# Moving one of the five score banks of an attention stage from the maxima tiles to the exponential tiles

## The chip, the cores and the metric

The kernel runs on one core of one Trainium2 chip. The metric is the device time of one execution in microseconds (us), the median of several runs. TensorE (PE; its weight loads, PEld, are listed by themselves), VectorE (DVE), ScalarE (ACT), GpSimd (POOL) and SyncE (SP) each run their own instructions in program order and wait for each other through semaphores. PSUM, into which PE writes its products, is eight banks of 128 partitions x 512 fp32.

## What is computed

Eight sequences of 512 positions with 256 features go through an attention layer and then through a mixture of experts. The part of the reference that matters here is the attention with 16 heads of 16 features:

```python
attn = softmax(einsum('bhid,bhjd->bhij', q, k) / sqrt(16))     # 8 x 16 heads of 512 x 512 scores
mod = attn * coh[..., None]
mod = mod / (mod.sum(-1, keepdims=True) + 1e-08)
mod = (1.0 - fi) * mod + fi * fa[:, None, :, None]
out = einsum('bhij,bhjd->bhid', mod, v)
x = x + out.reshape(...) @ Wout.T + bout
```

After it a gate picks two of eight experts for each row, three layers are computed for the picked ones, and the weighted results are added up.

## The kernel before, in words

`attention` (L180) holds the whole first half, `experts` (L976) the second. The change touches the first alone.

The attention stage is one hand-written sequence of steps s (L621, FIRST to LAST), 16 for each of the eight sequences ("batch" in the code), 128 in all; slot means the step's place within its sixteen (step 54 is slot 6). A step treats four heads of one block of 128 positions. Every head's scores are computed **twice**. An *A tile* (`a_tile`, L426) is a 128 x 512 block of scores with a query position per partition; DVE reduces it to the maximum of each row (`reduce_head`, L746). A *B tile* (`b_tile`, L437) is the transposed block, with the key position per partition, and the maximum already folded into the product; ACT takes its exponential into SBUF (`exps`, L691), and `pv` (L448) multiplies the result with the values. The maxima must be complete before a head's B tiles, so the A tiles run LEAD = 8 steps ahead: in step s PE makes the four B tiles of s and the four A tiles of s + 8. Steps -8 to -1 have A tiles alone (the lead-in, about 52 to 84 us), steps 120 to 127 have B tiles alone (about 629 to 656 us).

The tiles use rings of PSUM banks. A tile number `no` goes to bank `no % RING` of its ring, and PE waits, before it writes, until the tile RING places earlier has been read:

```python
if no >= A_RING:
    pe.wait_ge(a_read, no - A_RING + 1)      # a_tile, L429; the same with b_read and B_RING in b_tile, L440
```

`a_read` is raised by DVE's reduction (L750), `b_read` by ACT's exponential (L697). Before the change the A ring has three banks and the B ring two. Bank 5 gathers the `pv` products, banks 6 and 7 serve all other products of the stage.

PE's order in one step is (L621 to L629):

```python
scores(s, (0, 1))            # B0 A0 B1 A1, called the first pairs below
product(task(s, 0))          # another product of the stage, if PLAN has one here
pv(s - 1)                    # waits until all four exponentials of step s - 1 are done
scores(s, (2, 3))            # B2 A2 B3 A3, the second pairs
product(task(s, 1))
```

A B tile and the A tile that follows it use opposite halves of the array's rows, and start together when neither waits. PLAN (L110) gives the other product of each of the 16 steps, on either side: projections, the coherence layer, transposes, output and gate products. DVE's order (L951 to L969) is two reductions, what it has to take of side 0, two reductions, side 1, and in steps 5, 6, 7, 8, 9 and 11 a piece of the routing of the batch before (`route_batch`, L865), a chain of tiny dependent instructions; the piece of step 9 is the longest (L886 to L891) and ends in `both`, for which the `count` product of step 10 waits. ACT's order (L704 to L733) is two exponentials, side 0, the DMA of the maxima (L688) in every fourth step, the copy of the `pv` bank (L682), two exponentials, side 1.

Of the kernel before, what the change touches and what calls it, by code (L numbers as in the profile page):

```python
# [28 lines left out]
COUPLING = 0.3 * 0.7  # L29
KEEP = 1.0 - COUPLING  # L30
SCALE = 1.0 / float(HD) ** 0.5
A_RING, B_RING = 3, 2

TS = 256
TILES_MAX = 2 * T // TS + NX - 1
# [39 lines left out]
def program(nc, dram, out):  # L75
    with ExitStack() as ctx:
        def sb(name, shape, dt=F32):
            return ctx.enter_context(nc.sbuf_tensor(name, shape, dt))

        banks = [ctx.enter_context(nc.psum_tensor(f"bank{i}", [P, 512], F32)) for i in range(8)]  # L80
        w = {n: sb("w_" + n, INPUTS[n]) for n in ("ident", "count", "b1", "b2")}
        start, region = sb("start", [P, NX]), sb("region", [P, NX])
        expert = sb("expert", [P, TILES_MAX + 2], I32)
        first_row = sb("first_row", [P, TILES_MAX + 2], I32)
        raw = sb("raw", [P, 2, HALF])
        raw_in = [ctx.enter_context(nc.semaphore(n)) for n in ("raw_half0", "raw_half1")]

        xs = nc.dram_tensor("xs", [NX * CAP + TS, ROW], F32).ap()
        parts_dram = nc.dram_tensor("parts_dram", [2, 2 * E, S], F16).ap()
        attention(nc, dram, banks, w, start, region, expert, first_row, raw, raw_in, xs, parts_dram, out)  # L90
        with ExitStack() as own:
            def mine(name, shape, dt=F32):
                return own.enter_context(nc.sbuf_tensor(name, shape, dt))

            w["b3"] = mine("w_b3", INPUTS["b3"])

            split = (mine("w_hi", INPUTS["we"], F16), mine("w_lo", INPUTS["we"], F16))
            experts(nc, banks, dram, w, raw, split, raw_in, expert, first_row, xs, out)
# [81 lines left out]
def attention(nc, dram, banks, w, start, region, expert, first_row, raw, raw_in, xs, parts_dram, out):  # L180

    with ExitStack() as own:
# [3 lines left out]
        def sem(name):  # L186
            return own.enter_context(nc.semaphore(name))
# [74 lines left out]
        marked, placed, scattered = sem("marked"), sem("placed"), sem("scattered")  # L262
        rows_kept, ends_set, filled = sem("rows_kept"), sem("ends_set"), sem("filled")
        link = sem("link")
        a_bank, b_bank, pv_bank, misc = banks[0:3], banks[3:5], banks[5], banks[6:8]
        turned_shift = misc[1][0:G, 0:S // 2].bitcast(F16)
        block = own.enter_context(nc.Block())

# [1073 lines left out]
```

## Time and profile before

| | us |
|---|---|
| median of 3 runs (1194.12 to 1197.74) | 1197.56 |
| the profiled execution, its own time | 1197.49 |
| its span, first to last instruction | 1195.3 |
| A tiles alone | 51.9 to 84.3 |
| A and B tiles, steps 0 to 119 | 84.3 to 629 |
| B tiles alone, steps 120 to 127 | 629 to 656 |
| mean granted TensorE clock, share of full speed | 0.922 |

All times within a trace are us from the start of the span. A timeline row shows the start, the duration, the engine, the source line and the instruction; "x4" joins four instructions of the same kind that follow each other, and a bracket says how long the engine had been idle before and what ended that. A duration runs to the recorded end, and back-to-back instructions overlap a little, so that a run of several is shorter than the sum.

### The profile page before, as it was taken

The page shows a single profiled execution, that of the slowest core. Times are in us where ns is not written, and L with a number is a line of the kernel's source. Part 1 is how long each engine was busy: PE and PEld are TensorE (multiplying, and loading weights), DVE is VectorE, ACT ScalarE, POOL GpSimd, SP SyncE. Part 2 cuts the span into 40 slices and gives each one's busy share as a digit, 9 for nine tenths or more (in the row PEclk, how much of TensorE's full clock was granted, in tenths as well). Part 3 has the DMA queues.
Part 4 walks back from the last instruction along what each step waited for, and adds up shares of the span by engine and source line. Part 5 has one row for each costly group of instructions (what it writes and reads, how often), then busy time and mean ns, then how long its engine had stood idle before and what let it go on. Part 6 is the DMA issues. An engine that isn't in the chain of part 4 may idle for free. (4 is left out here: it accounts for less than half of the span.)

```text
span 1195.3 us, 25169 instructions
## 1 busy us (share of the span) xinstructions
PE 1012.8 (85%) x7550; PEld 619.5 (52%) x7551; DVE 782.9 (65%) x1696; ACT 541.4 (45%) x1097; POOL 542.1 (45%) x590
## 2 busy tenths in 40 slices
PE   3698998998989899897987414889999999999994
PEld 1242333333323343332432313778999899899983
DVE  5467777787777877778773434786666566555552
ACT  2107665665656646556456024553333333333331
POOL 3213122424324233231213122677777877787775
PEclk9769998999989989899889656999999999999997
DMA  4661250713507134063115226662323332332232
GB/s 136 106 98 36 51 92 1 127 53 91 90 7 137 37 92 70 5 122 108 38 37 194 95 78 211 195 182 49 55 39 52 54 54 38 53 54 49 42 54 27
DMA packets 74211, 92.93 MB, mean 78 GB/s; under 512 B 18824, under 2 KB 64672, under 8 KB 71968
## 3 DMA queue, kind: packets, MB, share of 16 engines
q1 hardware_dynamic: 55760, 59.39, 21.9%
q0 software_dynamic: 14304, 19.15, 10.0%
q10 hardware_dynamic: 4080, 13.53, 3.4%
q8 instruction: 39, 0.64, 0.2%
q14 instruction: 28, 0.23, 0.1%
HBM read 53.22 MB, written 38.68 MB: 77 GB/s over the span
## 5 line engine op out<-in xcount | busy, mean ns | idle before, releaser
L750 DVE TENSOR_REDUCE mx<-bank 128x1 f32<-128x512 f32 x512 | 325.5, 682 | 84.3 <-PE bank L434 81.8
L697 ACT ACTIVATE pr<-bank 128x512 f32<-128x512 f32 x512 | 277.3, 595 | 171.9 <-PE bank L445 168.3
L1249 POOL TENSOR_TENSOR hl<-hf,hh 128x256 f16<-128x256 f32 x316 | 240.4, 1193 | 127.9 <-DVE y_dest L1212 77.9
L1145 ACT ACTIVATE hf<-bank,w_b 128x256 f32<-128x256 f32 x316 | 132.4, 470 | 275.8 <-PE bank L1092 275.7
L1195 DVE CAST hh<-hf 128x256 f16<-128x256 f32 x316 | 168.4, 546 | 128.1 <-ACT hf L1145 122.1
L445 PE MATMUL bank<-q,k 49*128 49x512 f16 x512 | 174.9, 398 | 43.8 <-ACT pr L697 35.6
L434 PE MATMUL bank<-k,q 48*128 48x512 f16 x512 | 179.4, 407 | 24.1 <-DVE mx L750 22.0
L1092 PE MATMUL bank<-hh,w_lo 128*128 128x256 f16 x624 | 170.1, 273 | 0.0
L1092 PE MATMUL bank<-hl,w_hi 128*128 128x256 f16 x624 | 170.1, 273 | 0.0
L1092 PE MATMUL bank<-hh,w_hi 128*128 128x256 f16 x624 | 170.1, 273 | 0.0
L445 PEld LDWEIGHTS bank<-q,k 49*128 49x128 f16 x512 | 36.2, 94 | 223.5 <-ACT pr L697 165.1
L459 PE MATMUL bank<-pr,v 128*17 128x512 f32 x1024 | 141.1, 624 | 1.2 <-ACT pr L697 1.2
L1255 POOL DMA_INDIRECT out<-y,y_dest x78 | 123.7, 1586 | 22.8 <-issue 18.4
L356 POOL CAST parts<-full 128x512 f16<-128x512 f32 x32 | 19.5, 609 | 211.5 <-ACT full L654 211.5
L1092 PE MATMUL bank<-xh,w_hi 128*128 128x256 f16 x320 | 91.5, 286 | 20.7 <-DVE w_lo L1216 19.2
L1092 PE MATMUL bank<-xh,w_lo 128*128 128x256 f16 x320 | 91.6, 286 | 0.0
L1092 PE MATMUL bank<-xl,w_hi 128*128 128x256 f16 x320 | 91.6, 286 | 0.0
L380 POOL DMA_INDIRECT xs<-rows,slot x64 | 62.6, 978 | 59.3 <-DVE rows L898 41.4
L1106 PE MATMUL bank<-w_hi,hh 128*128 x312 | 85.1, 273 | 1.6 <-DVE y L1204 1.2
L1106 PE MATMUL bank<-w_lo,hh 128*128 x312 | 85.1, 273 | 0.0
L1106 PE MATMUL bank<-w_hi,hl 128*128 x312 | 85.0, 273 | 0.0
L1092 PEld LDWEIGHTS bank<-hh,w_lo 128*128 x624 | 61.0, 98 | 7.1
(224 smaller groups left out, 1538.6 us busy)
## 6 DMA issues: line engine op xcount, KB each, us to landing
raw<-in_we ACTq DMA_DIRECT2D x12, 1024.0 KB, 4.7
x_tile<-xs SPq DMA_DIRECT2D x41, 256.0 KB, 3.0
parts_dram<-parts SPq DMA_DIRECT2D x16, 512.0 KB
xs<-pads SPq DMA_DIRECT2D x8, 816.0 KB, 9.5
q<-parts_dram SPq DMA_DIRECT2D x48, 128.0 KB, 6.7
k<-parts_dram SPq DMA_DIRECT2D x48, 128.0 KB, 7.0
xT<-in_xT SPq DMA_DIRECT2D x8, 512.0 KB, 4.0
xr<-in_x SPq DMA_DIRECT2D x8, 512.0 KB, 4.7
```

Of the source, the lines that this page charges most:

```text
L380: pool.indirect_dma_start(out=xs, out_offset=bass.IndirectOffsetOnAxis(ap=slot[:, i, t:t + 1], axis=0), in_=rows[:, t, :], in_offset=None) ...
L434: nc.tensor.matmul(a_bank[no % A_RING][:, :], q[r, par, h // 2, at * P:(at + 1) * P], k[r, par, h // 2, :], start=True, stop=True).then_in ...
L445: nc.tensor.matmul(b_bank[no % B_RING][:, :], k[r, par, h // 2, at * P:(at + 1) * P], q[r, par, h // 2, :], start=True, stop=True).then_in ...
L459: last = nc.tensor.matmul(pv_bank[HW * h:HW * h + SUM + 1, :], v[:, par, jt, g * G + h, :], pr[:, jt, h, :], start=(jt == 0), stop=(jt == ...
L697: nc.scalar.activation(pr[:, s % TT, n, :], b_bank[no % B_RING][:, :], ACT.Exp, scale=SCALE).then_inc(b_read, 1)
L750: V.tensor_reduce(mx[:, g % 2, s % TT, c:c + 1], a_bank[no % A_RING][:, :], X, ALU.max).then_inc(a_read, 1)
L1092: last = nc.tensor.matmul(out, weights(name, part, e, k, c), a, start=(k == 0 and n == 0), stop=(k == K - 1 and n == 2), skip_group_check= ...
L1106: last = nc.tensor.matmul(y_bank[:, s * E:(s + 1) * E], a, weights("w3", part, e, k, slice(0, E)), start=(k == 0 and n == 0), stop=(k == M ...
L1145: nc.scalar.activation(hf[which][:, par, m, :], layer[which][m // 2][:, m % 2 * TS:(m % 2 + 1) * TS], ACT.Relu, bias=bias[which][:, bass.d ...
L1195: nc.vector.tensor_copy(hh[which][:, par, m, :], hf[which][:, par, m, :]).then_inc(hi[which], 1)
L1249: nc.gpsimd.tensor_tensor(hl[which][:, par, m, :], hf[which][:, par, m, :], hh[which][:, par, m, :], ALU.subtract).then_inc(lo[which], 1)
L1255: pool.indirect_dma_start(out=out, out_offset=bass.IndirectOffsetOnAxis(ap=y_dest[:, s:s + 1], axis=0), in_=y[:, s, :], in_offset=None, co ...
```

## The change

A_RING becomes 2 and B_RING 3, and the slice of banks follows: banks 0 and 1 for the A tiles, banks 2, 3 and 4 for the B tiles. Nothing else is changed; no instruction is added, removed or reordered. PE now waits at an A tile for the reduction of the A tile two places earlier, and at a B tile for the exponential of the B tile three places earlier.

```diff
-A_RING, B_RING = 3, 2
+A_RING, B_RING = 2, 3
...
-        a_bank, b_bank, pv_bank, misc = banks[0:3], banks[3:5], banks[5], banks[6:8]
+        a_bank, b_bank, pv_bank, misc = banks[0:2], banks[2:5], banks[5], banks[6:8]
```

## Rows read from the trace of the kernel before

**Rows 1.** The page, part 1: busy us (share of the span) xinstructions.

```profile
PE 1012.8 (85%) x7550; PEld 619.5 (52%) x7551; DVE 782.9 (65%) x1696; ACT 541.4 (45%) x1097; POOL 542.1 (45%) x590
```

**Rows 2.** Windows: stretch, length, busy us of each engine, granted clock, DMA.

```profile
core 0: us, PE busy (x) PEld busy (x) DVE busy (x) ACT busy (x) POOL busy (x), PEclk, DMA share, GB/s
...
51.90:84.30 32.40, 29.63 (x118) 12.04 (x118) 21.47 (x37) 2.06 (x3) 5.29 (x6) 0.62 0.43 78
...
297.00:368.00 71.00, 63.17 (x422) 24.13 (x420) 55.09 (x126) 42.47 (x85) 23.92 (x22) 0.95 0.35 71
...
629.00:656.00 27.00, 20.02 (x128) 6.00 (x130) 8.99 (x37) 19.91 (x38) 9.07 (x9) 0.99 0.50 193
```

**Rows 3.** Waits, 84 to 656 us: total us, times, longest.

```profile
PEld bank L445 <- ACT pr L697: 165.1, 260, 1.9
...
PEld bank L434 <- DVE mx L750: 23.4, 10, 3.4
...
PE bank L434 <- DVE mx L750: 19.4, 8, 3.1
```

**Rows 4.** Timeline, the second pairs of step 49 and the first of step 50.

```profile
303.73 2.22 ACT L697 ACTIVATE pr<-bank 128x512 f32<-128x512 f32 x4 [1.23 <-PE bank L445]
303.76 2.48 DVE L750 TENSOR_REDUCE mx<-bank 128x1 f32<-128x512 f32 x4 [0.17 <-PE bank L434]
...
304.38 0.39 PE L445 MATMUL bank<-q,k 49*128 49x512 f16 x1 [0.47 <-ACT pr L697]
...
304.87 0.39 PE L434 MATMUL bank<-k,q 48*128 48x512 f16 x1
...
305.19 0.39 PE L512 MATMUL bank<-x_high,wc1x_hi 128*128 128x512 f16 x1
```

**Rows 5.** Timeline, the first pairs of step 49.

```profile
299.97 1.29 DVE L750 TENSOR_REDUCE mx<-bank 128x1 f32<-128x512 f32 x2 [0.91 <-PE bank L434]
...
301.42 0.39 PE L434 MATMUL bank<-k,q 48*128 48x512 f16 x1
```

**Rows 6.** Timeline, step 54 (slot 6).

```profile
324.08 2.67 DVE L750 TENSOR_REDUCE mx<-bank 128x1 f32<-128x512 f32 x4
...
325.25 0.39 PE L434 MATMUL bank<-k,q 48*128 48x512 f16 x1
```

**Rows 7.** Timeline, step 58 and the start of step 59.

```profile
341.88 0.39 PE L434 MATMUL bank<-k,q 48*128 48x512 f16 x1
...
344.97 2.47 DVE L750 TENSOR_REDUCE mx<-bank 128x1 f32<-128x512 f32 x4
...
345.71 0.39 PE L434 MATMUL bank<-k,q 48*128 48x512 f16 x1 [3.15 <-DVE mx L750]
...
346.42 1.85 PE L610 MATMUL bank<-both,ones 128*128 128x32 f32 x8
...
350.22 1.91 PE L459 MATMUL bank<-pr,v 128*17 128x512 f32 x8
```

**Rows 8.** Timeline, lead-in with A tiles alone, one run of eight.

```profile
61.04 4.87 DVE L750 TENSOR_REDUCE mx<-bank 128x1 f32<-128x512 f32 x8 [2.12 <-PE bank L434]
...
61.79 2.99 PE L434 MATMUL bank<-k,q 48*128 48x512 f16 x5 [0.36 <-DVE mx L750]
64.72 0.61 PE L512 MATMUL bank<-x_high,wk_hi 128*128 128x512 f16 x1
```

**Rows 9.** Timeline, steps 122 to 126, B tiles alone.

```profile
639.11 1.04 PE L610 MATMUL bank<-both,ones 128*128 128x32 f32 x8
...
646.92 0.66 PE L518 MATMUL bank<-w_ident,oT 128*128 128x128 f32 x4
...
649.57 0.88 PE L445 MATMUL bank<-q,k 49*128 49x512 f16 x2 [0.69 <-ACT pr L697]
650.37 1.05 PE L459 MATMUL bank<-pr,v 128*17 128x512 f32 x8
...
648.92 2.23 ACT L697 ACTIVATE pr<-bank 128x512 f32<-128x512 f32 x4 [1.23 <-PE bank L445]
```

## The prediction

> **What bounds the kernel now.** I read the page's busy shares first: PE is busy 85% of the span, DVE 65%, ACT and POOL 45% [rows 1]. A share over the whole span says little here, so the windows come next. In a middle batch, 71 us, PE is busy 63.2, DVE 55.1 and ACT 42.5; in the lead-in, with A tiles alone, the granted clock is 0.62; in the last steps, with B tiles alone, DVE has 9.0 us of work in 27 and ACT 19.9 [rows 2]. The experts' half has its own use of the banks and is not touched. PE is the engine through which everything in the stage passes, in program order, so what counts is where PE waits.
>
> The waits seem to speak for the change. PE's weight load of a B tile waits 260 times for an exponential, 165.1 us in total; that of an A tile waits 10 times for a reduction, 23.4 us [rows 3]. But a wait is named after whoever ended last. Whether taking ACT's away gains anything depends on when DVE's would have ended, and only the timeline shows that.
>
> **A normal turn from second pairs to first pairs.** In step 49 the exponentials of B2 and B3 start at 303.73, and the reductions of A2 and A3 at 303.76 [rows 4]. In runs of back-to-back reductions the first ends 0.69 after the start and each later one 0.60 after the one before (0.69 + 0.60 = 1.29 for two [rows 5], + 3 x 0.60 = 2.49 for four [rows 4]). So the reductions end at 304.45 and 305.05. The next B0 starts at 304.38 and the pair B1/A1 at 304.87 [rows 4]: PE now moves at ACT's pace of one exponential per 0.49. With rings of 2 and 3, B0 no longer waits, but A0 waits for the reduction of A2 (304.45) and A1 for that of A3 (305.05). A tile starts 0.05 after its release (345.71 after a reduction that ends at 344.97 + 0.69 = 345.66 [rows 7]), so A1 starts at 305.10 instead of 304.87: **0.23 later**, and the product behind it, now at 305.19, moves with it. The third B bank gives nothing back, because PE runs in order: B1 stands behind A0, and the next product behind A1. ACT and DVE gain nothing either: the four exponentials and the four reductions there are already back to back [rows 4]. The next reductions start fresh after PE's next tiles, so this is added to the path each time. Laying the same ruler on every pair of steps 0 to 119, I count 34 such places: usually slots 2, 4, 8 (or 7) and 15, five or six in the first batch and in the seventh. 34 x 0.235 = **+8.0 us**.
>
> **Places with another sum.** (a) Where ACT began late, the third B bank pays. In step 49 the reductions run from 299.97 and end at 301.26, so A1 could start at 301.31 instead of 301.42 [rows 5], 0.1 earlier. Slots 1 and 9 are like this, 12 places: **-1.1**. (b) In slot 6 DVE is late with the routing. Step 54's four reductions start at 324.08; the second ends at 325.37, and A3, now at 325.25, has to wait until 325.42 [rows 6]: 0.17 in each of five batches, and 0.1 once in the first, **+1.0**.
>
> (c) **DVE's long holds.** In slot 9 the routing keeps DVE until 344.97. PE has placed A2 at 341.88 and stands with A3, the third tile ahead, until 345.71 [rows 7]. With two banks it already stands at A2, which starts at 345.71, and A3 has to wait for the second reduction, 344.97 + 1.29 + 0.05 = 346.31: 0.60 later. `count` and the next tiles stand behind it, and DVE's own next piece needs `count`. This happens once in each of batches 2 to 6, twice in the seventh and once in the eighth: 8 x 0.60 = **+4.8**. In these places DVE is the one that is behind, so neighbouring 0.24s of the seventh batch are already in the 0.60 and are not counted.
>
> **Lead-in.** A tiles alone, four runs, each of which PE ends by waiting for a reduction; one is eight tiles long, 61.04 to 65.91 on DVE, and the product behind it starts at 64.72 [rows 8]. The last tile now waits one reduction longer, 0.61: 4 x 0.61 = **+2.4**. Here two banks also slow DVE. At this clock a matmul takes 0.61 [rows 8], so two tiles through two banks take 0.69 + 0.05 + 0.61 + 0.05 = 1.40 against 1.20 now, 0.1 a tile, on some eight tiles: **+0.8**. Its bounds are 0 (the ends of matmuls are modelled) and 0.1 x 20.
>
> **Last steps, B tiles alone.** This is the gain. B1 of step 126 waits now for the exponential of B3: the pair is 649.57 and 650.06 (the row of two is 0.88 long, a matmul 0.39), `pv` at 650.37 [rows 9]. With three banks B0 starts at once and B1 when B2's exponential ends (648.92 + 0.59 = 649.51). `pv` then waits for that of B3, 648.92 + 0.59 + 0.49 = 650.00, so it starts at 650.05: 0.32 gained where `pv` follows directly; 0.49 where another product stands between, as in step 125 (646.92 [rows 9]). Steps 120, 124, 126, 127 give 0.32 and 121, 125 give 0.49; what 122 would give ends in front of `count`, which waits for DVE. Together **-2.3**.
>
> **The sum**: 8.0 - 1.1 + 1.0 + 4.8 + 2.4 + 0.8 - 2.3 = +13.6 us. Against the profiled execution's own time, 1197.49 (its span and 2.2 around it), that gives 1211.1; the median of the runs is 0.07 away from it, so I say **1211**. Beyond the stage nothing changes: its last `pv` is PE's, and what follows is a chain.
>
> The ruler was read off places that exist. What it cannot show is whether a lag is taken back later. If it is after every hold, terms (b), (c) and the lead-in go, -9.0, which leaves 1202; that is the lower bound. The upper bound comes from the clock, below.
>
> **The rules that speak here.** The rows say that the pace of the wait is the slower reader's. The Trainium skill's Perfetto Trace Analysis page (Consistent bubbles, under Optimization Strategy) says that a gap that comes back on the engine that should be saturated can mean too few buffers for the next tile. By it the 260 waits on ACT would ask for just this third B bank, and by it alone the sum would have the other sign; the first rival below takes that up.
>
> **Rivals.**
> *Faster (0.05).* The B waits are the bound and the A waits do not take their place. Place: the turn from second to first pairs, some ten times a batch; price: up to 0.49 each, as in the last steps, 8 x 10 x 0.49 = 39 us, so 1158. It decides if a bank becomes free at least 0.23 before the recorded end of its reduction. For it: 165 us of waits. Against it: A3 at 345.71, 0.05 after the recorded end [rows 7].
> *The lag is absorbed (0.07).* DVE has 16 us of 71 free [rows 2] and could catch up, and gains and losses cancel: -1.1 - 2.3 against part of 8.0, within 1197 to 1201. Against it: after nearly every pair DVE's next run starts with a wait for PE, so a late PE moves it too.
> *The clock (0.10).* After the hold of rows 7 PE runs at the lower of its two levels, 1.2 GHz: `count`'s eight matmuls take 1.85 against 1.04 at 2.4 GHz [rows 7, 9] and `pv` 1.91 against 1.05 [rows 7, 9], with the pairs and transposes between about 3 us a stretch. The clock fell after PE had stood for 3.2 us. The holds now start a tile earlier. If they, and seven that keep full speed today, add one such stretch per batch, that is 7 x 3 = +20 on top of the sum, 1231. The Trainium skill's page TensorE: Matmul & The Clock Gate (A second HAM failure mode: psum-queue depth-cycling) tells of a kernel whose short stops between groups of matmuls, as it cycles through banks, make the clock swing. By that rule more and shorter waits are the danger. Against this rival: middle batches hold 0.95 with ten or more stops each [rows 2].
>
> **How the numbers follow.** The forecast case has 0.78: its terms were each read at both ends of a wait. Its own range is 1203 to 1217. The range given reaches a little further towards the clock's case, 1203 to 1222. A change below 0.3% (3.6 us) could not be told from none in this kernel. Faster by more than that: 0.05. Same: 0.07, the absorbed case. Slower: 0.78 + 0.10 = 0.88.
>
> **What would show it.** In the changed profile: PEld L445 <- ACT waits fall from 165.1 us to a small rest, and L434 <- DVE takes their place with some hundreds of waits instead of 10. In a turn such as step 49's, B0 comes right after the second pairs, A1 0.05 after the second reduction. In slot 10 the wait of PE moves from A3 to A2 and the product after it starts 0.6 later relative to DVE. A middle batch grows from about 71.2 to 72.8, the lead-in by 3, the last steps shrink by 2. Wrong would be: A tiles that start earlier than the recorded end of the reduction two tiles back; a middle batch no longer than now; a granted clock below 0.93 in a middle batch.

## The result, and the profile after

| | before | after |
|---|---|---|
| median, us | 1195.84 (1191.96 to 1197.74, 4 runs) | 1218.09 (1215.21 to 1219.84, 4 runs) |
| ratio, 95% interval | | 1.0188 (1.0153 to 1.0223) |
| profiled execution: its time, its span | 1197.49, 1195.3 | 1218.01, 1215.9 |
| mean granted TensorE clock | 0.922 | 0.915 |

The change makes the kernel slower by 22 us. The forecast was 13.6, so 1211; 1218 lies inside the stated range of 1203 to 1222, but just above the 1203 to 1217 that the forecast gave as the range of its own case. Executions more than 1.5% above the fastest of their kernel are left out of every ratio, here and in the experiments, where three of them took 1610, 1993 and 3430 us for a reason that no trace shows. Part 1 of the page after, which answers to [rows 1]:

```profile
PE 1056.1 (87%) x7550; PEld 633.1 (52%) x7551; DVE 782.6 (64%) x1696; ACT 535.1 (44%) x1097; POOL 541.2 (45%) x590
```

DVE and POOL work as long as before and ACT 6 us less; PE is "busy" 43 us longer with the same instructions. Most of that is not longer work but less overlap. A B tile and the A tile behind it started within 0.05 us of each other in 463 of the 480 pairs of steps 0 to 119, and do so in 295 now. From step 0 to step 127 the A and B tiles add up to 395 us before and 397 after, but they cover 180 us of time before and 218 after. PE's time without a matmul in the steps fell at the same time, from 65 us to 42, and its stands of more than 0.3 us from 82 to 49. The waits of the stage after (84 to 677 us; us in total, times, longest), against [rows 3]:

```profile
PEld bank L434 <- DVE mx L750: 105.4, 173, 3.7
...
PEld bank L445 <- issue: 78.0, 93, 1.7
PEld bank L445 <- ACT pr L697: 60.2, 78, 1.7
...
PE bank L434 <- DVE mx L750: 36.5, 45, 3.4
```

The weight loads of B tiles that wait for ACT went from 260 to 78, and 173 of A tiles that wait for DVE, where there were 10, took their place. The forecast's sign was a small rest and some hundreds; the rest is not so small. The waits that are gone save nothing, as the turn of steps 49 and 50 shows, which answers to [rows 4] (timeline: start, duration, engine, line):

```profile
307.78 1.89 DVE L750 TENSOR_REDUCE mx<-bank 128x1 f32<-128x512 f32 x3
...
307.55 0.59 PE L445 MATMUL bank<-q,k 49*128 49x512 f16 x2
308.53 0.39 PE L434 MATMUL bank<-k,q 48*128 48x512 f16 x1 [0.38 <-DVE mx L750]
308.75 0.38 PE L445 MATMUL bank<-q,k 49*128 49x512 f16 x1
309.13 0.39 PE L434 MATMUL bank<-k,q 48*128 48x512 f16 x1
309.45 0.39 PE L512 MATMUL bank<-x_high,wc1x_hi 128*128 128x512 f16 x1
```

B0 does come right after B3 (the row of two L445), but A0 waits until the end of the first reduction and 0.06 more (307.78 + 0.69 + 0.06 = 308.53) and A1 likewise for the second (307.78 + 1.29 + 0.06 = 309.13). The reductions start at 307.78 and the product behind the pairs at 309.45: 1.67 apart, 1.43 before (303.76 to 305.19 [rows 4]). That is the 0.24.

The hold of slot 10 answers to [rows 7]:

```profile
348.52 0.39 PE L445 MATMUL bank<-q,k 49*128 49x512 f16 x1
352.27 0.39 PE L434 MATMUL bank<-k,q 48*128 48x512 f16 x1 [3.36 <-DVE mx L750]
352.49 0.38 PE L445 MATMUL bank<-q,k 49*128 49x512 f16 x1
352.86 0.39 PE L434 MATMUL bank<-k,q 48*128 48x512 f16 x1
353.18 0.41 PE L608 MATMUL bank<-both,w_tri 128*128 128x32 f32 x2
```

PE stands at A2 now (352.27) and A3 comes 0.59 after it (352.86). The rest of the loss is not in such rows but in the clock. Windows of the kernel after (stretch, length, busy us of PE, PEld, DVE, ACT, POOL, granted clock, DMA), one in slot 7 (step 55), one around slot 6 of the seventh batch (steps 101 to 103) and one in the last steps:

```profile
332.70:336.80 4.10, 4.10 (x18) 0.90 (x18) 2.25 (x8) 1.71 (x3) 0.13 (x1) 0.58 0.00 0
...
552.00:572.00 20.00, 17.20 (x88) 6.70 (x86) 13.65 (x30) 9.17 (x22) 2.37 (x1) 0.74 0.45 160
657.30:671.00 13.70, 12.98 (x50) 3.21 (x49) 2.06 (x11) 6.80 (x14) 7.82 (x8) 0.50 0.77 301
```

Before, slot 7 of the same batch ran at the full clock, and the last steps at 0.99 [rows 2]:

```profile
327.90:330.50 2.60, 2.60 (x18) 0.75 (x18) 2.39 (x8) 1.77 (x3) 0.54 (x1) 1.00 0.00 0
```

The last of the forecast's signs of being wrong was a granted clock below 0.93 in a middle batch. From the first B tile of a batch to that of the next, batches 2 to 6 have 0.93 to 0.96 (0.93 to 0.98 before), but the seventh has 0.89 (531.48 to 610.00) where it had 0.95. In its step 102 PE stands at an A tile before the clock falls, longer than it did before the change (timelines, before and after; the number in the bracket is the stand):

```profile
550.65 0.39 PE L434 MATMUL bank<-k,q 48*128 48x512 f16 x1 [1.27 <-DVE mx L750]
```

```profile
562.64 0.60 PE L434 MATMUL bank<-k,q 48*128 48x512 f16 x1 [2.06 <-DVE mx L750]
```

Measured in the same way, batches 2 to 6 grew by 1.5 to 3.3 us and the seventh by 6.4; the forecast had 1.6.

### The profile page after: what moved, and what is told of

Read it like the earlier page. It is cut to its first block and busy times, and to the rows that moved or that the text cites. A ratio compares the mean times of both kernels' runs of the same rounds, so it can differ in the third digit from the quotient of the medians.

```text
span 1215.9 us, 25169 instructions
## 1 busy us (share of the span) xinstructions
PE 1056.1 (87%) x7550; PEld 633.1 (52%) x7551; DVE 782.6 (64%) x1696; ACT 535.1 (44%) x1097; POOL 541.2 (45%) x590
## 3 DMA queue, kind: packets, MB, share of 16 engines
q1 hardware_dynamic: 55760, 59.39, 21.5%
## 5 line engine op out<-in xcount | busy, mean ns | idle before, releaser
L697 ACT ACTIVATE pr<-bank 128x512 f32<-128x512 f32 x512 | 270.7, 600 | 188.0 <-PE bank L445 187.7
L445 PE MATMUL bank<-q,k 49*128 49x512 f16 x512 | 168.7, 401 | 2.9 <-ACT pr L697 2.9
L459 PE MATMUL bank<-pr,v 128*17 128x512 f32 x1024 | 145.8, 644 | 1.7 <-ACT pr L697 1.2
L1255 POOL DMA_INDIRECT out<-y,y_dest x78 | 123.6, 1585 | 22.5 <-issue 17.5
L445 PEld LDWEIGHTS bank<-q,k 49*128 49x128 f16 x512 | 36.0, 95 | 147.2 <-issue 78.0
L434 PEld LDWEIGHTS bank<-k,q 48*128 48x128 f16 x512 | 36.8, 94 | 123.1 <-DVE mx L750 118.7
```

What stands on the lines that cost most here:

```text
L434: nc.tensor.matmul(a_bank[no % A_RING][:, :], q[r, par, h // 2, at * P:(at + 1) * P], k[r, par, h // 2, :], start=True, stop=True).then_in ...
L445: nc.tensor.matmul(b_bank[no % B_RING][:, :], k[r, par, h // 2, at * P:(at + 1) * P], q[r, par, h // 2, :], start=True, stop=True).then_in ...
L459: last = nc.tensor.matmul(pv_bank[HW * h:HW * h + SUM + 1, :], v[:, par, jt, g * G + h, :], pr[:, jt, h, :], start=(jt == 0), stop=(jt == ...
L697: nc.scalar.activation(pr[:, s % TT, n, :], b_bank[no % B_RING][:, :], ACT.Exp, scale=SCALE).then_inc(b_read, 1)
L1255: pool.indirect_dma_start(out=out, out_offset=bass.IndirectOffsetOnAxis(ap=y_dest[:, s:s + 1], axis=0), in_=y[:, s, :], in_offset=None, co ...
```

## The books, step by step

The measure in this section is the distance from one step's B2 to the next step's, in one trace against the trace before. For the fourth batch (steps 48 to 63), in us; a slot's number stands over the way into its B2:

```
slot        0     1     2     3     4     5     6     7     8     9    10    11    12    13    14    15    sum
after     0.00 -0.11 +0.24  0.00 +0.24 +0.03 -0.31 +2.13 +0.23 -0.07 +0.15 +0.27 +0.20 +0.04  0.00 +0.24  +3.28
ring22    +1.63 +0.01 +0.24  0.00 +0.24 +0.03 -0.03 +1.55 +0.45  0.00 +0.07 +0.80 +0.23 +0.04 +5.96 +1.52
half23    +1.63 -0.48 -0.30  0.00 -0.30 -0.49 -0.31 +1.61 -0.30 -0.48  0.00 -0.44 -0.41 -0.49 +6.25 +0.11
fill32c   0.00  0.00  0.00  0.00  0.00  0.00  0.00  0.00  0.00  0.00  0.00 -2.71 -0.41  0.00  0.00  0.00  -3.12
fill23h   0.00 -0.10 +0.24  0.00 +0.24 +0.03 -0.31 +2.70 +0.23 -0.07 +0.15 -2.19 -0.41 +0.04  0.00 +0.24  +0.79
```

The rows below the first belong to the experiments. In batches 2 to 6 of every trace with the same rings and reductions the small numbers return to within 0.03, except right beside a stretch at the lower clock; those of about 1.3 and more come with such a stretch or with one that is gone, or, in the two slower groups of experiments, with slot 14. Slots 2, 4, 8 and 15 are the forecast's turns, 0.24 each, and slots 1 and 9 its gains of 0.1, which came out as 0.1 and 0.08. In batches 3 and 5 slot 7 costs 0.49, and there the clock is full; in batches 2, 4 and 6 it costs 2.1, with a low stretch of 3.4 us.

## The experiments

Ten runs in four groups; a ratio always compares with the kernel before as it ran in the same group. The groups are ring22, half32, half23 and fill32; again23, fill23 and fill32b; fill23g; fill23h and fill32c. In the first two every kernel took some 5% longer, that of before among them (1255 and 1259 against 1198): in every kept trace batches 2 to 7 lose 4.5 to 6.3 us in slot 14 there, most of them with a long low stretch in slots 14 to 0. Whole times are therefore compared within a group alone.

**1. Which bank is it? ring22, half32, half23.** ring22 has two banks for either kind and leaves one unused:

```diff
-A_RING, B_RING = 3, 2
+A_RING, B_RING = 2, 2
...
-a_bank, b_bank, pv_bank, misc = banks[0:3], banks[3:5], banks[5], banks[6:8]
+a_bank, b_bank, pv_bank, misc = banks[0:2], banks[2:4], banks[5], banks[6:8]
```

> Two banks for the A tiles, two for the B tiles, one bank unused. Theory (the second A bank's lack sets the pace, the third B bank pays only in a few places): the normal turns stay 0.24 us later as in the changed kernel, and the third B bank's small gains (0.1 in slots 1 and 9, 0.32 to 0.49 a step at the end) are missing: 0 to 6 us slower than the changed kernel, so about 1218 to 1224. Rival (the third B bank does harm itself: it lets B0 start before A0, so that the pairs no longer run together on the two halves of the array): the pairs run together again, and it is faster than the changed kernel by 3 us or more, below 1215.

Measured: 1283.17 against 1254.75, ratio 1.021 (1.0149 to 1.0271), where the change had 1.0188. The 1218 to 1224 expected do not hold in this slower group; by the ratios ring22 is 0.2% above the changed kernel, as expected, but inside the noise. With the third B bank taken away as well, the same turn (timeline) reads:

```profile
328.24 0.38 PE L445 MATMUL bank<-q,k 49*128 49x512 f16 x1
329.08 0.39 PE L445 MATMUL bank<-q,k 49*128 49x512 f16 x1 [0.47 <-ACT pr L697]
329.21 0.39 PE L434 MATMUL bank<-k,q 48*128 48x512 f16 x1
329.57 0.39 PE L445 MATMUL bank<-q,k 49*128 49x512 f16 x1
329.81 0.39 PE L434 MATMUL bank<-k,q 48*128 48x512 f16 x1
```

B3 to A1 takes 1.57 here and 309.13 - 307.55 = 1.58 in the changed kernel, with B0 early or late. So the lost A bank makes the 0.24, and the split pairs do no harm to this distance. What the third B bank pays is the difference of the rows "after" and "ring22": 0.1 in slots 1 and 9, 0.28 in slot 6, less 0.08 in slot 10. In whole times the two kernels cannot be told apart.

half32 is the kernel before, half23 the changed one, each with the second half of every maximum left out, so that a reduction is shorter than an exponential:

```diff
-a_bank[no % A_RING][:, :], X, ALU.max)
+a_bank[no % A_RING][:, 0:256], X, ALU.max)
```

> The kernel before, with each maximum taken over columns 0 to 255 of the tile alone (the other half of the maximum is left out). A reduction should fall from 0.68 to about 0.42 us. It is the partner of half23. Both theories: the turns stay tied to the exponentials, so little is gained, only the waits after DVE's holds get shorter: 1180 to 1196.

> The changed kernel, with each maximum taken over columns 0 to 255 alone (the other half is left out). Theory (PE moves at the pace of the slower reader, so the third B bank pays as soon as a reduction is shorter than an exponential): in a normal turn A1 waits for neither, B1 starts at the end of B2's exponential, some 0.25 us earlier than in half32; ten turns a batch and the end give half23 12 to 22 us less than half32. Rival (a third bank for the B tiles is worth nothing, or costs by the split pairs): half23 equals half32 or is slower.

Measured: 1233.26 and 1206.34 against 1254.75, ratios 0.983 (0.9793 to 0.9867) and 0.9633 (0.9598 to 0.9667). A reduction takes 0.42. half32 gained 21.5 us, more than the 1.5 to 17.5 expected; in its trace B2 of step 0 alone comes 13.6 sooner than in the trace before, with 3 us at the lower clock ahead of it instead of 30. **half23 is 26.9 us faster than half32, more than the 12 to 22 expected: the same move of a bank that cost 22 us now gains.** Not all of the 26.9 is the bank's, as half23's steps have 124 us at the lower clock and half32's 144. The turn in half32 and then in half23 (timelines):

```profile
308.86 0.38 PE L445 MATMUL bank<-q,k 49*128 49x512 f16 x1
309.70 0.39 PE L445 MATMUL bank<-q,k 49*128 49x512 f16 x1 [0.47 <-ACT pr L697]
...
310.20 0.39 PE L434 MATMUL bank<-k,q 48*128 48x512 f16 x1
310.51 0.39 PE L512 MATMUL bank<-x_high,wc1x_hi 128*128 128x512 f16 x1
```

```profile
296.11 0.59 PE L445 MATMUL bank<-q,k 49*128 49x512 f16 x2
296.82 0.39 PE L434 MATMUL bank<-k,q 48*128 48x512 f16 x1
297.05 0.38 PE L445 MATMUL bank<-q,k 49*128 49x512 f16 x1
297.15 0.39 PE L434 MATMUL bank<-k,q 48*128 48x512 f16 x1
297.47 0.39 PE L512 MATMUL bank<-x_high,wc1x_hi 128*128 128x512 f16 x1
```

From B3 to the next product: 1.65 in half32, 1.36 in half23; and the books have -0.30 to -0.49 in eight slots (1, 2, 4, 5, 6, 8, 9 and 13) in which half32 has 0.00. These make 3.2 us in the fourth batch; with six such batches and the 3.6 of the first, about 22 us are the bank's in batches 1 to 7. With a reduction of 0.42 against an exponential of 0.59 the extra bank pays on ACT's side; at 0.68 against 0.59 it pays on DVE's. Where between the two it turns was not run.

**2. Is the rest the clock? fill32, again23, fill23.** fill32 adds matmuls to the kernel before where PE stands in slot 10:

```diff
+def filler(s):
+    t = task(s, 1)
+    if t is None or t[0] != "count" or s // SLOTS not in range(1, 7):
+        return
+    side, no = USES[t]
+    after(pe, misc_read[side], no)
+    for _ in range(12):
+        nc.tensor.matmul(misc[side][:, :], high["wq"][:, 0, 0:P], x_high[:, s // SLOTS % 2, 0, :],
+                         start=True, stop=True, skip_group_check=True)
...
                     if scored(s):
                         b_tile(s, n)
+                    if n == 3:
+                        filler(s)
```

fill23 is the same on the changed kernel, with `n == 2`; again23 is the changed kernel itself.

> The kernel before with 12 matmuls of 128 x 128 x 512 f16 added in slot 10 of batches 2 to 7, into the bank that count is about to overwrite, between B3 and A3, where PE stands for some 3 us until DVE's hold is over. Theory (the stand brings the lower clock, which lasts 3.4 to 10.2 us after each hold and costs some 3 us each time; this is also where the changed kernel lost the part that the bank waits do not explain): the granted clock stays at full speed over slots 10 and 11, and the kernel gets 12 to 20 us faster than before. Rival (the clock does not depend on this stand): no low stretch goes away, the time is that of before or up to 6 us more.

> The changed kernel once more, next to its own variants on one chip. It was 1.0188 of the kernel before. Both theories: 1.012 to 1.025 of it here too, with the same 0.24 us in slots 2, 4, 8 and 15 whatever the chip's clock does.

> The changed kernel with the 12 matmuls of 128 x 128 x 512 f16 added in slot 10 of batches 2 to 7, after B2 and before A2, where it stands now. Theory (what the changed kernel lost beyond the bank waits is time at the lower clock): slots 11 and 12 run at the full clock, 10 to 20 us less than the changed kernel; the 0.24 us of slots 2, 4, 8, 15 stay, so it remains 8 to 20 us above fill32. Rival (with the full clock the banks make no difference): fill23 equals fill32 within 3 us.

> The kernel before with the 12 matmuls in slot 10, once more and next to fill23 on the same chip. Theory: 1 to 2% less than the kernel before, the fastest of the three rings with full computation. Rival: its gain on the first chip was that chip's, and here it is within 0.3% of the kernel before.

| | median | kernel before, same group | ratio (95%) |
|---|---|---|---|
| fill32 | 1239.08 | 1254.75 | 0.9866 (0.9831 to 0.9902) |
| fill32b | 1237.34 | 1258.57 | 0.9837 (0.9793 to 0.9882) |
| again23 | 1285.52 | 1258.57 | 1.0104 (1.0032 to 1.0176) |
| fill23 | 1258.24 | 1258.57 | 0.9998 (0.9964 to 1.0033) |

again23's six runs fall into two threes, 1269.14 to 1280.2 and 1290.85 to 1291.2. Its ratio rests on the lower three and lies just below the 1.012 to 1.025 expected, with an interval that reaches into it; by the medians of all it is 1.021. Its small numbers in the books are those of the first comparison. Filling the stand takes 14 us off the median of the lower three, as expected (10 to 20), and 27 off the median of all six. It leaves fill23 21 us above fill32b, just over the 8 to 20 that I gave: the full clock in slots 10 to 12 does not make the two rings equal. The 21 are not the banks' alone: fill23's steps have 126 us at the lower clock, fill32b's 97.

The same kernel in the fourth group, fill32c:

> The kernel before with the 12 matmuls in slot 10, a third time. If this call gets a chip on which the kernel before takes about 1197 us, like the one of the first comparison: Theory: slots 11 and 12 of six batches 2.2 to 3.0 us shorter, 13 to 18 us in all, 1.1 to 1.5% below the kernel before. Rival (it pays only on chips with a lower mean clock): within 0.3%.

Measured: 1181.55 against 1198.65, ratio 0.9848 (0.9802 to 0.9895). The books' row is all zeros but for slots 11 and 12, -3.12 in this batch and -16.9 in the six batches with the added matmuls (13 to 18 expected). Two low stretches elsewhere take 3.3 back, so that from step 0's B2 to step 127's it is 13.8 us shorter. Its timeline, and then a window over the same stretch:

```profile
337.22 0.39 PE L434 MATMUL bank<-k,q 48*128 48x512 f16 x1 [0.45 <-DVE mx L762]
337.53 0.41 PE L608 MATMUL bank<-both,w_tri 128*128 128x32 f32 x2
337.78 1.04 PE L610 MATMUL bank<-both,ones 128*128 128x32 f32 x8
...
339.87 1.05 PE L459 MATMUL bank<-pr,v 128*17 128x512 f32 x8
```

```profile
326.00:345.00 19.00, 17.98 (x122) 7.10 (x122) 16.74 (x44) 10.93 (x21) 6.08 (x7) 1.00 0.01 2
```

`count` takes 1.04 and `pv` 1.05, against 1.85 and 1.91 [rows 7]. A3 comes no sooner (3.84 after B2, 3.83 before), and everything behind it does. This is the version that beats both kernels, and it computes everything.

**3. Slot 7: fill23g, fill23h.** fill23 with 3, then 10, more matmuls in slot 6 between B3 and A3, in front of `gate`'s sixteen matmuls of eight columns (the filler's condition widened to `gate`, its count 3 or 10).

> fill23 with 3 more matmuls of 128 x 128 x 512 f16 per batch, in slot 6 between B3 and A3 (into the bank that gate is about to overwrite), where the changed kernel stands 0.37 us for DVE. In fill23 a low stretch of 3.4 us in slot 7 follows in most batches and costs about 2.1 us each. Theory (the short stands that two A banks add around gate's tiny matmuls bring this stretch): slot 6 takes 0.3 more and slot 7 about 1.6 less per batch, so 5 to 8 us less than fill23, which was equal to the kernel before. Rival (gate's sixteen tiny matmuls bring it, whatever stands beside them, or these three are too few): slot 7 keeps its 2.1, the kernel gets 2 us slower than fill23.

> fill23 with 10 instead of 3 more matmuls per batch in slot 6, between B3 and A3. They take 10 x 0.21 = 2.1 us, 0.4 of it in the stand. Theory (gate's tiny matmuls leave the array so little to do that the clock falls behind them, and full work beside them prevents it): slots 6 and 7 together are 1.7 longer by the work and 2.1 to 2.8 shorter by the clock, no low stretch in slots 6 and 7 of batches 2 to 6. Rival (the stretch hangs on something else, such as the placing in time): it stays, and slots 6 and 7 together are 1.7 or more longer than in fill23.

Measured: fill23g 1205.71 against 1198.43, 1.0102 (1.0012 to 1.0191); fill23h 1210.08 against 1198.65, 1.0107 (1.0074 to 1.0141). With three, slot 7 costs 2.8 in four of the five batches 2 to 6 and 4.0 in the other, and its stretch is still there: the theory of the short stands, as I had put it, failed. The kept traces are against it too. The 0.37 is the distance from the start of B3 to that of A3, which a matmul of 0.38 fills, and in the 9 us before each of the changed kernel's three stretches PE never stands for more than 0.25; in half23 and fill32, where B3 and A3 start together in slot 6, the stretch comes in three and in two of the five batches. With ten there is no low stretch left from 90 to 556 us (window):

```profile
100.00:556.00 456.00, 438.74 (x2819) 169.22 (x2815) 343.31 (x765) 265.28 (x534) 139.99 (x131) 1.00 0.35 73
```

Slot 7 then costs 2.70, of which the added work is 10 x 0.21 and the banks 0.49 (with some 0.1 left over). That is 0.1 less than with three, where 0.4 to 1.1 less were expected for slots 6 and 7. So full work in front of `gate` does prevent the stretch, but costs more than it saves: 2.70 in each batch, against 2.13 with the stretch and 0.49 without in the changed kernel. Why the kernels with two A banks have it more often stays open. Of batches 2 to 6 they have it in 24 of 30 (after 3, again23 5, ring22 5, half23 3, fill23 3, fill23g 5, without fill23h), the five kernels with three A banks in 5 of 25 (before 0, half32 2, fill32 2, fill32b 1, fill32c 0). Ten matmuls prevent it in either cause.

## Why the prediction was right, and where it was short

**The pace of the slower reader: right.** 0.235 was the term; 0.22 to 0.24 is measured, in 31 places for the 34 that were counted. ring22 shows that it is the A bank alone, half23 that its sign hangs on which reader is slower. The two ratios of half23 and half32 are also the answer to the rival that the B waits were the bound: they were in name, and are in fact with a reduction of 0.42.

**The holds (+4.8): right.** The clean price is fill23h against fill32c in slots 10 and 11: 0.15 + 0.52 = 0.67 in the fourth batch and 0.65 to 0.68 in batches 2 to 6, for 0.60. PE did move from A3 to A2.

**Slots 6 and 7: right in sum.** -0.31 + 0.49 + 0.23 for slot 8 is 0.41; I had 0.17 + 0.24. A batch with nothing else in it costs 1.69 (the row "after", with slot 7 at 0.49 and slots 10 to 12 at 0.67) against 1.53 by the forecast's terms (4 x 0.235 - 2 x 0.09 + 0.17 + 0.60).

**The end (-2.3): the mechanism right, the term hidden by the clock.** In fill23g, whose clock was full there, steps 121 to 127 give -0.48, -0.32, +0.32, -0.32, -0.49, -0.32, -0.32, the forecast's 0.49s and 0.32s; with the changed kernel's own -0.35 for step 120 that is -2.3. But in the changed kernel's trace 13.7 us of these steps ran at 0.50, and steps 120 to 127 cost 2.4 instead.

**The lead-in (+3.2): there, smaller, and covered by the clock.** From the first A tile to B2 of step 0 the changed kernel's trace is 1.3 shorter, 35.86 against 37.11 (it starts 0.8 sooner and arrives 2.07 sooner). But it has 20 us of this part at the lower clock, and the trace before has 30. The other kernels tell what the banks do there. With three A banks and whole reductions the part takes 31.56, 33.40, 35.49 and 37.11 with 10.2, 16.2, 22.8 and 29.6 us at the lower clock (fill32, fill32c, fill32b, before): on a line of 0.29 per us, within 0.2, which gives 34.5 at 20 us. The five kernels with two A banks and three B banks take 35.72 to 37.74 with 19.9 to 20.4, so 1.3 to 3.1 more. The line is an estimate from four traces; by it the term was real and mostly put too high.

**The clock: the step that was mis-sized.** I gave it as a rival, at 0.10 and +20, and put nothing of it into the sum. It came in part. From step 0's B2 to step 127's the traces differ by 22.9 us. The record of the granted clock has 55 us at the lower level between steps 1 and 127 before and 82 after, 27 more, in 12 stretches instead of 8: new are three of 3.4 us in slot 7, one of 10.2 in step 102 and 13.7 in the last steps, and some went. A stretch of 3.4 costs 2.13 - 0.49 = 1.64, or 0.48 per us; the 13.7 of the last steps cost 2.4 + 2.3 = 4.7, or 0.35 per us. As an estimate, the clock makes 11 to 13 of the 22.9 and the banks 10 to 12, where the forecast without its lead-in was 10.4. The spans differ by 20.6: the 22.9, less 1.3 in the lead-in, 0.8 ahead of it and 0.3 behind the last step.

So the mechanism of the banks was right, and the time lies in the range by luck in part. As much again as the banks cost came from the clock, which the sum had at nothing, and the lead-in's term was covered by another clock there. 1218 is above the forecast's own 1217 and inside only because the range reached a little towards the clock's case, 9 us short of that case's 1231. (The lower bound, too, was worked out as 1202 and given as 1203.) The clock's case should have stood beside the sum as a term of some size. Its reasoning held in one place that the runs show, step 102, where PE stands 2.06 us instead of 1.27; the stretches in slot 7 follow no stand above 0.25 us, and their cause is open.

The Trainium skill's rule of Perfetto Trace Analysis (Consistent bubbles), by which the 260 waits on ACT would ask for the third B bank, did not decide: bubbles were there, and the bank that they seemed to ask for moved them and made the kernel slower. By the Trainium skill's page TensorE: Matmul & The Clock Gate (A second HAM failure mode: psum-queue depth-cycling) frequent short stops between groups of matmuls make the clock swing. The clock did swing more, 12 low stretches against 8, but not by that count: PE's stands of more than 0.3 us fell from 82 to 49.

## What to carry to other kernels

When two readers empty tiles that one engine makes in turn, the ring of the slower reader sets the pace; give it the spare buffer, and find it by when each reader would have been done, not by whose name stands in the waits. Lay the new wait on the recorded ends of the readers, place by place: that came out to 0.01 us in the turns and to 0.08 in the holds. Then ask what the clock will do, as it made half of the loss here. PE's busy share is no measure of either: it rose because tiles that had run together no longer did. Where a long wait of PE is followed by matmuls at the lower clock, matmuls of no use in that wait, into a bank that is about to be overwritten, gained 1.3 to 1.6% here in three comparisons.

## What was not expected of the hardware

In the kernel before, after a stand of 3.2 us PE runs at 1.2 GHz for 6.8 us (346.1 to 352.9, granted 0.53 in the window of 345.7 to 352.9), long after it is busy again; twelve matmuls in the stand prevent that (granted 1.00 from 326 to 345 in fill32c). In the slower groups PE's weight loads within `gx`'s 24 small matmuls have gaps of 0.6 us that end in "issue", and ACT stands for 3.8 us before its next exponential (364.05 to 367.88 in fill32), in the steps where POOL scatters rows; the clock then falls for up to 17 us. As an example, fill32's weight loads there:

```profile
365.57 0.10 PEld L512 LDWEIGHTS bank<-wgr_hi,x_low 128*128 128x128 f16 x1 [0.65 <-issue]
...
366.29 0.10 PEld L512 LDWEIGHTS bank<-wgr_lo,x_high 128*128 128x128 f16 x1 [0.61 <-issue]
```

The loss in slot 14 is in every kept trace of those two groups, and the kernel before took 5% longer there too; its cause was not tried. A DVE instruction on 128 x 4 numbers (L764) took 2.33 beside a GpSimd instruction of 2.37 in step 101 of the changed kernel, where in the kernel before it took 0.17 and the next one (L765), 0.17 in the changed kernel, took 2.22, which is part of why PE stands in step 102.

```profile
558.74 2.33 DVE L764 TENSOR_SCALAR t<-ms 128x4 int32<-128x4 int32 x1
...
558.68 2.37 POOL L416 TENSOR_TENSOR xr<-xr,w_bo 128x1024 f32<-128x1024 f32 x1 [16.24 <-DMA xr<-in_x]
```
